# Filler products on TensorE in the three plain gather stages of a four-layer graph network

## The reference, cut to what matters

```
h = maximum(layernorm(x), 0);  x = x + layer(h)
L0: per edge, MLP(h[dst], edge_attr)            -> segment_sum over dst
L1: per edge, (A[type] @ h)[src]                -> segment_sum over dst -> GRU cell
L2: per edge, tanh MLP of p1[src], p1[dst], basis -> segment_sum over dst
L3: conv, twice: h[src] -> segment_sum over dst -> mean, two products, (relu)
```

## Time and profile before

| | us |
|---|---|
| median of 3 runs (12554.08 to 12559.82) | 12558.62 |
| the profiled execution | 12561.67 |
| its span, first to last instruction | 12559.8 |
| PE busy | 6173.3 (49%) |
| PEld busy | 3820.2 (30%) |
| DVE busy | 4382.5 (35%) |
| ACT busy | 2380.1 (19%) |
| POOL busy | 6399.4 (51%) |
| indirect DMAs | 6656, four stages of 1664 |
| mean granted clock of TensorE | 0.672 of full |

### The profile page before, as it was taken

How to read it: one execution, slowest core, us unless ns; L and a number is a source line. 1 busy time by engine, 2 the same in 40 slices (tenths; PEclk the granted TensorE clock), 3 DMA queues, 4 the chain that set the end, 5 groups by cost and what they waited for, 6 DMA issues and landing times. The chain is left out here.

```text
span 12559.8 us, 146068 instructions
## 1 busy us (share of the span) xinstructions
PE 6173.3 (49%) x34361; PEld 3820.2 (30%) x34522; DVE 4382.5 (35%) x11997; ACT 2380.1 (19%) x4618; POOL 6399.4 (51%) x6688
## 2 busy tenths in 40 slices
PE   3999996233333337888888882233332321111111
PEld 2777772122222222333333331222222211111111
DVE  4888873122222224555555552111111111111111
ACT  1888871000000002222222220000000000000000
POOL 1000001666666655555555555666666656666666
PEclk9999995555555558888889885555555555555555
DMA  3222222111111111121111121111111111111111
GB/s 112 79 79 79 79 65 91 23 25 24 25 25 25 25 23 44 45 46 46 46 46 46 46 46 19 23 23 23 24 23 23 23 21 24 24 24 24 24 24 24
DMA packets 498703, 488.54 MB, mean 39 GB/s; under 512 B 242267, under 2 KB 296352, under 8 KB 498080
## 3 DMA queue, kind: packets, MB, share of 16 engines
q0 software_dynamic: 212992, 218.53, 9.4%
q1 hardware_dynamic: 285664, 269.47, 7.3%
HBM read 427.04 MB, written 61.15 MB: 39 GB/s over the span
## 5 line engine op out<-in xcount | busy, mean ns | idle before, releaser
L1349 PE MATMUL ps<-outs,mov 128*64 128x64 f32 x9984 | 1298.8, 313 | 2377.2 <-issue 1010.4
L624 POOL DMA_INDIRECT outs<-tab_u,idx x1664 | 1606.1, 965 | 1294.5 <-DVE idx L877 825.5
L801 DVE TENSOR_TENSOR acc<-acc,ps 64x64 f32 (+1 forms) x1664 | 350.0, 210 | 5382.0 <-remote 4354.4
L624 POOL DMA_INDIRECT mov<-tab_msg,idx x1664 | 1582.6, 951 | 1151.5 <-issue 505.7
L624 POOL DMA_INDIRECT mov<-tab_h,idx x1664 | 1582.5, 951 | 977.3 <-issue 493.4
L624 POOL DMA_INDIRECT mov<-tab_q,idx x1664 | 1579.5, 949 | 879.5 <-issue 509.3
L1349 PEld LDWEIGHTS ps<-outs,mov 128*64 128x64 f32 x9984 | 1133.7, 220 | 2602.9 <-issue 2251.2
L901 DVE TENSOR_TENSOR scr<-ps,scr 128x512 f32<-128x512 f32 x1664 | 1067.8, 685 | 403.9 <-PE ps L1478 159.4
L1486 PE MATMUL ps<-scr,w_bas 128*64 128x512 f32 x3328 | 1085.8, 736 | 0.0
L608 POOL MEMSET acc<- 64x13312 f32 x1 | 11.2, 11186 | 1675.9 <-ACT mov L1138 1675.9
L1478 PE MATMUL ps<-bas,pair 128*128 128x512 bf16 x1503 | 581.0, 439 | 566.6 <-DVE scr L901 502.2
(11 more groups left out here) (211 smaller groups left out, 8735.5 us busy)
## 6 DMA issues: line engine op xcount, KB each, us to landing
mov<-in_dst_row SPq DMA_DIRECT2D x832, 128.0 KB, 2.6
mov<-in_ea_T SPq DMA_DIRECT2D x416, 128.0 KB, 2.5
tab_msg<-outs SPq DMA_DIRECT2D x104, 256.0 KB, 2.0
mov<-tab_msg,idx POOLq DMA_INDIRECT x1664
outs<-tab_u,idx POOLq DMA_INDIRECT x1664
mov<-tab_h,idx POOLq DMA_INDIRECT x1664
mov<-tab_q,idx POOLq DMA_INDIRECT x1664
win<-tab_g SPq DMA_DIRECT2D x416, 32.0 KB, 2.3
```

Source lines behind the costliest of these rows:

```text
L624: nc.gpsimd.indirect_dma_start(out=gat(e, u)[:, k, :], out_offset=None, in_=table, in_offset=bass.IndirectOffsetOnAxis(ap=idx[:, u, k:k + ...
L801: nc.vector.tensor_tensor(into, into, bank(banks[u % len(banks)])[0:rows, 0:W], ALU.add) \
L1349: last = mm(bank(banks[u % len(banks)])[0:width, 0:W], values(u)[:, k, :], sel(e, u)[:, k, :], start=k == 0, stop=k == TL - 1)
```

## The change

In the plain gather stages PE gets 14 more products after each chunk's sum (`keep_busy`): `pair[:, 0, :]` (128x128) by `bas[:, 0, :]` (128x512), bf16, into all 512 columns of PSUM bank 2, which nothing reads. They wait for no semaphore and raise none. To free bank 2, the two transposes that wrote it write the second half of bank 0 instead, and ACT reads them there.

```diff
+FILL = 14
@@ ACT, gru_chain
-                nc.scalar.activation(hT[0:D, 1, 0:SN], bank(2)[0:D, 0:SN], ACT.Copy).then_inc(f.sems["lifted"], 1)
+                nc.scalar.activation(hT[0:D, 1, 0:SN], bank(0)[0:D, SN:2 * SN], ACT.Copy).then_inc(f.sems["lifted"], 1)
@@ ACT, conv_chain
-                nc.scalar.activation(tT[:, 0, 0:SN], bank(2)[:, 0:SN], ACT.Copy).then_inc(f.sems["lifted"], 1)
+                nc.scalar.activation(tT[:, 0, 0:SN], bank(0)[:, SN:2 * SN], ACT.Copy).then_inc(f.sems["lifted"], 1)
@@ PE
+            def keep_busy(it, u, _):
+
+                for _ in range(FILL):
+                    mm(bank(2), pair[:, 0, :], bas[:, 0, :], start=True, stop=True)
+
             def plain(e, pieces):
                 with pe.Fori(0, P) as p:
-                    chunk_loop(pe, [(0, sum_stage(e, p, D, lambda u: gat(e, u), gathered_here(e, p), range(4, 8)))],
+                    chunk_loop(pe, [(0, sum_stage(e, p, D, lambda u: gat(e, u), gathered_here(e, p), range(4, 8))),
+                                    (0, keep_busy)],
                                nodes=(WAIT_TURNS, pieces(pe.snap(p * SG))))
@@ PE, turn_next (e=1)
-                        last = nc.tensor.transpose(bank(2)[0:D, k * P128:(k + 1) * P128], next_h[:, k, :], ident[:, :])
+                        last = nc.tensor.transpose(bank(0)[0:D, SN + k * P128:SN + (k + 1) * P128], next_h[:, k, :], ident[:, :])
@@ PE, turn_hid (e=3)
-                        last = nc.tensor.transpose(bank(2)[:, k * P128:(k + 1) * P128], hidn[:, k, :], ident[:, :])
+                        last = nc.tensor.transpose(bank(0)[:, SN + k * P128:SN + (k + 1) * P128], hidn[:, k, :], ident[:, :])
```

## The result

The changed kernel takes 13055.67 us (median of 4 runs, 13047.62 to 13084.9) against 12559.03 of before, a ratio of 1.0401 with the interval 1.0383 to 1.0419. The forecast was slower, 13530, with a range of 12250 to 15000. The sign held. The loss is 497 us where 972 was forecast. Ratios here are of fast runs alone, and one of the fourth group's seven runs of the kernel before, 16963.91 us, was slow and is left out of them.

What follows compares the result with a forecast made beforehand. Bound: PE's late signals delay additions and stop POOL. 4.99+4.5/2.8 = 6.60 us a chunk, taken with e=2's 6.81 as 6.70; 1248 chunks make 8362 against 7390.4, +972, so 13530 us, range 12250 to 15000.

Steps and rivals of the forecast that it cites:

- Late signals are the bound: Plain gather stages: PE's "done" reaches others late while POOL issues, so POOL stops; without this 1160 us less.
- The mechanism, records before time: Gather stages: the fillers' 28 more records a chunk, 46.9 for 18.9, decide by shortening POOL's bursts, not their PE time.
- A: Theory that PE's records pass at about one per POOL DMA, so their count decides; 13400 to 14000 for e8_narrow28b.
- chunks a burst: POOL's bursts in the gather stages: 133 records over 46.9 a chunk give 2.8 chunks before POOL stops.
- The middle with e=2: Gather stages' time a chunk: 6.70 us, the middle of the summed 6.60 and stage e=2's 6.81.
- The count of about 115 as a limit: PE in gather stages: takes about 115 records (106 to 116) after POOL's restart before it crawls.
- Where 9 to 12 chunks fit: POOL's bursts in the gather stages before the change: said to hold 9 to 12 chunks.
- rival 4: Gather stages: records don't count, fillers only slow catching up after a stop; +200 to +500 us, 12900, chance 0.13.
- Fillers behind the last sum: End of each gather stage: 3x3.4 = 10 us at most, largely hidden by additions, taken as 0.
- Rival 1: Gather stages: signals are late because PE idles at low clock; fillers cure it, 1160 us go, 11400, chance 0.15.
- Rival 2: Gather stages: warm clock alone makes sums after a stop cheaper, 0.2 us a chunk; -250, 12310, chance 0.07.
- Rival 3: Gather stages: idle PE absorbs the fillers and records without semaphores don't count; no change, 12560, chance 0.12.

Runs made afterwards that it cites:

- fourth group: Last set of follow-up runs, e11_upper_rest8 and e12_change_rest2, on a chip where the kernel before took 12565.45 us (7 runs).
- e6_narrow14b: Changed kernel with its 14 fillers a chunk cut from 512 to 64 columns; 13026.82 us, ratio 1.0375 to the kernel before.
- e12_change_rest2: Changed kernel, all fillers kept, with POOL resting for one memset after every second chunk; 12609.37 us, ratio 1.004 to the kernel before.
- e8_narrow28b: Changed kernel with 28 fillers of 64 columns a chunk in place of 14 of 512; 13138.54 us, ratio 1.0536 to the kernel before.
- second group: Follow-up runs of the change again, of 14 narrow fillers and of 3 long float32 fillers, where the kernel before took 12556.57 us; ratios 1.0413, 1.0375, 1.0239.
- e1_banks: Changed kernel with no filler products, only the moved banks; 10839.95 us on the chip where the kernel before took 10839.22.
- e9_upper: Kernel before with sums of e=1, 3 and 4 from the upper 16 bits, 8 records in place of 16; 12376.77 us, ratio 0.9925.
- e10_pause4: Kernel before with POOL resting for two memsets after every fourth chunk of e=1, 3 and 4; 12360.01 us, ratio 0.9912.
- e11_upper_rest8: Kernel before with sums from the upper 16 bits and POOL resting for two memsets after every eighth chunk; 12416.17 us, ratio 0.9877.

## Why the prediction was right, and where it was off

*Late signals are the bound.* Right, and now shown by a run: on a chip without them the same kernel takes 10839 us.

*The mechanism, records before time.* Right in the main. The change and e6_narrow14b start crawling at 101 and 108 records with PE times a factor of two apart, and e12_change_rest2 takes nearly the whole loss away by breaks of POOL alone. But PE's time, or the clock that goes with it, has a share: in e=3 and e=4 about 40% of the loss is gone when the same number of fillers takes half the time. And e8_narrow28b, with twice the records, lost 670 us where A's forecast comes to 840 to 1440.

*The size.* The measured 13056 lies at the very edge of the forecast's own range (13050 to 15290), and the loss is half of the one forecast. The term that was mis-sized is *chunks a burst*, 2.8; it measured 3.4 to 3.7. The prediction allowed 115 records from POOL's restart and 18 before its second DMA. In the stop shown above some 14 ran between the release and the restart and 135 between the restart and the crawl, 149 for 133. More pass one by one while PE crawls, which the sum left out: 3.5 chunks of 46.9 are 164 records a burst, not 133. The stop of 4.5 us was right. With 3.5 chunks, 4.99+4.5/3.5 is 6.28, and the stages took 6.23 to 6.32. In the forecast's terms that is 400 us less than with 6.60.

*The middle with e=2.* It added 0.10 us a chunk, another 125 us too much. The prediction took e=2's 6.81 us as partly its own work; where signals aren't late, e=2 takes 5.48, so that it was mostly the same holdup, in a stage that stops every second chunk, and no measure.

That the lower bound of 6.32 us a chunk met the measured value is luck: it was made of stops of 3.71 us and 2.8 chunks, where 4.5 and 3.5 were measured.

*The count of about 115 as a limit.* From a clean start it is 101 to 127, but it is no constant: about 63 records are pending when PE crawls, and the rest of the count has passed already. The prediction held that a queue of 64 could be a part of it but not all; by the rows of the second group the pending ones alone fill about as many places.

*Where 9 to 12 chunks fit.* Wrong as a mean. It was read from the start of e=4; over the stages bursts before were 4.6 to 6.8 chunks. The prediction's own 133 records over 18.9 give 7. The forecast didn't rest on it, but rival 4 did.

*The moved banks*: 0, as taken (0.9999, 0.999 to 1.0009, though on the chip without holdup). *Fillers behind the last sum*: 0 was taken, 10 at most. It was some 46 for the three stages: a stage now ends with PE a ring behind, so that its last sums are still to come when POOL is done.

*The clock.* PE climbed to the high level, as expected: the granted clock rose from 0.52 to 0.84 in e=1, and a sum took 0.68 us against 1.11. The Trainium skill ("TensorE: Matmul & The Clock Gate", Why this matters for your kernels) advises to leave TensorE no long gaps between matmuls, so that the clock stays at the high level, and the trace agrees. No gain in time is seen, since the sums were off the path: e6_narrow14b, at a clock of 0.53 to 0.57, lost nearly as much in all as the change at 0.82 to 0.85. For e=1 alone, where it lost twice as much, a worth of the clock isn't excluded.

*Rival 1* (busy PE cures it) is refuted twice: the change has the busy PE and longer lags, and the chip without lags has the idle one. Rival 2 fails with it, as no stage got faster.

*Rival 3* (no change) is what the chip without late signals shows, 0.9999 to 1.0004 with fillers of three kinds, and only that chip. The change's own filler was not run there.

*Rival 4* (slower by 200 to 500 us, only the catching up) has the measured 497 us in its range, so the time alone doesn't rule it out. Its signs do: it wanted bursts of 6 to 8 chunks and fillers back to back, and there were 3.4 to 3.7 and crawling ones.

## What to carry to other kernels

Where POOL issues indirect DMAs without a break, look for instructions with "issue" as the reason of a gap of 1 to 3 us, and for waits that end only when POOL stops; there, an instruction of another engine can have a price beside its time (here some 0.38 us for 28 records of PE, by e6_narrow14b). Count instructions before filling an idle engine, and before trusting that work off the path is free. A short break of POOL can pay for itself (0.991 here), but it was only run where signals were late; where they are not, one would expect it to cost its length. Measure the kernel before on each chip that a comparison uses: one and the same program took 10839 and 12559 us.

## What the runs showed of the hardware

- The same kernel took 10839 us on one chip, 12469 on another, and 12557 to 12565 in the other groups and the first runs. On the first no sum's signal was over 2 us late (e1_banks), where up to 39 us were seen before; POOL's pace (1.248 us a DMA) was the same. What makes the chips differ is open.
- While POOL issues, about 63 records of PE and PEld can be pending (63, 63 and 64 in three kernels); then PE crawls. Once signals are late, about one record passes a DMA: 16 in 17 DMAs, and 8 in 9 (e9_upper).
- PE was released some 3.4 us into the stop of POOL that is shown. A rest of 2.06 us between DMAs was enough for 96 records (e12_change_rest2, e=3) and not wholly for the 94 of e=1, where sums still ended 9.7 us behind their DMAs; one of 3.2 us was enough for 80 (e10_pause4).
- DVE is held up too once PE has few records (e11_upper_rest8): gaps of 4.00 and 7.52 us, with register instructions 1.4 us apart.
